# Layer 1's experts: from all eight on every row to the two chosen, on ranked tiles of 128 rows

## The chip, the cores and the metric

One NeuronCore of a Trainium2 chip runs the whole program. The metric is the device time of one execution in microseconds (us). Five engines work side by side and wait for each other through semaphores: TensorE (PE, matmuls), VectorE (DVE), ScalarE (ACT), GpSimd (POOL) and SyncE (SP, which mostly issues DMAs). Sixteen DMA engines move data between device memory (HBM) and the on-chip SBUF.

## What is computed

Two transformer layers on x of shape [2, 2048, 256], float32. Layer 0 is softmax attention with 16 heads of 16, then a mixture of 16 experts with limited capacity. Layer 1 is a linear attention, and then the block of which this change rewrites one half:

```
qkv = x @ W_qkv + b_qkv                    # W_qkv [256, 768]
attn_out = softmax(q k^T / 4) v            # 16 heads of 16, 2048 keys
gate = softmax(x @ W_gate + b_gate)        # 8 experts
top_g, top_i = top_k(gate, 2)
combine = sum(one_hot(top_i) * top_g)      # zero for 6 of the 8 experts
expert_out = einsum('bsd,edf->bsef', x, W_experts) + b_experts
return attn_out + einsum('bsef,bse->bsf', expert_out, combine)
```

Here x is the layernormed and modulated input h, and the result is added to the residual after a multiplication by a gate. No row is dropped in layer 1: each takes its two experts, however many rows choose the same one.

## The kernel before, in words

The 4096 rows are 32 tiles of 128 (NT), or 8 groups of 512 (N = B * GPB: two batches of four groups). The program is a row of blocks, each ended by a barrier of all engines: the projection of layer 0 (`project_layer0`), its attention (`softmax_attention`), its experts (`finish_layer0`), the linear attention, then `project_layer1_ffn` and the second `softmax_attention` (called with `last=True`).

`project_layer1_ffn` is the block that changes. Per group of 512 rows PE computes the logits of the gate (L1881), q and k (L1887, into the four banks of `qk_ps`), v (L1892), the biases of the experts weighted by the shares (L1898, L1903), and then for each of the four tiles all eight experts, in pairs of 512 columns (L1918). To keep float32 accuracy in the one-pass format (fp32r), each pair takes three products (high by high, high by low, low by high) for each half of the 256 inputs: 96 matmuls of 512 columns a group. DVE multiplies each expert's result by its share and adds it to `acc` (L2005, 32 a group), POOL multiplies by the gate of the residual and adds to x (L1865, L1867). The next group's layernorm is turned (`ln_tensor`, L141) before the last tile. ACT and DVE split q and k in a high and a low part (L175, L180), and SP stores them (`split_store`, L195) and v (`store_values`, L203) in HBM; at the last four groups SP also loads ahead the first keys (L322) and queries (L312) of the attention.

After the last group come `first_maxima` on PE (L252) and `take_first_maxima` on DVE (L261): 48 steps of two matmuls of 512 columns (50 rows each) and a maximum over 1024 columns, on a ring of two. They give the row maxima with which the attention starts.

`softmax_attention` runs 32 steps (two batches, four head groups, four query groups) of 16 key tiles. Per key tile PE does 4 score matmuls (L803), 4 for the maxima two steps ahead (L791) and 8 for the values (L818), ACT 4 exponentials (L873), DVE 2 maxima (L892). POOL is free but for adding the finished attention rows to x (L768, L770).

`finish_layer0` already has a form of what the change brings: rows scattered in HBM by expert with indirect DMAs on POOL (L1139), then 32 items of 256 rows. Each is loaded by SP (L1116, ring of four), turned by PE (L1221), shifted by ACT (L1317), multiplied (L1230, L1239) with weights at fixed addresses, scaled by DVE and stored; the linear attention gathers the rows again (L1513).

## Time and profile before

| | |
|---|---|
| median of 3 runs | 3696.02 us (3692.02 to 3698.27) |
| profiled execution, its own time | 3697.96 us |
| its span, first to last instruction | 3696.2 us |
| PE busy | 3494.7 us (95%) |
| DVE busy | 3144.4 us (85%) |
| ACT busy | 2532.1 us (69%) |
| POOL busy | 355.3 us (10%) |
| mean granted clock of PE | 0.957 of full speed |

Busy time is per engine; engines overlap, so the numbers don't add up to the span. The changed block runs from 2034.9 us to 2422.5 us of the span; the second attention fills the rest.

### The profile page before, as it was taken

Reading aid. Unit: us, or ns where it says so; the run is one execution under the profiler, and the core shown is the slowest. Engines: PE = TensorE matmul, PEld = TensorE weight load, DVE = VectorE, ACT = ScalarE, POOL = GpSimd, SP = SyncE. Lnnn points to the kernel's source line nnn. Section 1 sums busy time; section 2 is a strip of 40 time slices with the busy share of each in tenths; the row PEclk is TensorE's granted clock in tenths of the full one; section 3 lists DMA queues with packets and bytes.
Section 4 is the critical chain, followed back from the end, with each engine's and each line's share of the span. In section 5 each row is a group of like instructions: output and inputs, shape, how many; then the busy total and the mean of one; then the engine's idle time right before and its main releaser. Section 6 shows DMA issues by size and latency. Waiting matters only on the chain. (4 is left out here: it accounts for less than half of the span.)

```text
span 3696.2 us, 75111 instructions
## 1 busy us (share of the span) xinstructions
PE 3494.7 (95%) x29968; PEld 1634.9 (44%) x29968; DVE 3144.4 (85%) x4194; ACT 2532.1 (69%) x4681; POOL 355.3 (10%) x271
## 2 busy tenths in 40 slices
PE   9899999999999998677898899889999999999998
PEld 5433333333333333565777677533333333333333
DVE  8899999999999992524666676899999999999993
ACT  3188888888888886232322333168888888888887
POOL 4410000000000000341221121100000011000001
PEclk9699999999999999798999899789999999999999
DMA  9442020211202003152000325121220212202001
GB/s 258 121 137 38 14 42 15 37 31 26 37 20 37 14 11 99 63 188 82 27 23 12 91 57 104 41 42 22 34 37 18 38 42 59 39 14 42 15 16 45
DMA packets 279102, 193.17 MB, mean 52 GB/s; under 512 B 202573, under 2 KB 234230, under 8 KB 274384
## 3 DMA queue, kind: packets, MB, share of 16 engines
q1 hardware_dynamic: 268896, 158.40, 20.1%
q0 software_dynamic: 8400, 28.91, 2.2%
q8 instruction: 213, 3.49, 0.4%
q10 hardware_dynamic: 1504, 1.64, 0.1%
q14 instruction: 89, 0.73, 0.1%
HBM read 107.54 MB, written 81.79 MB: 51 GB/s over the span
## 5 line engine op out<-in xcount | busy, mean ns | idle before, releaser
L873 ACT ACTIVATE att_l_probs<-att_l_s_ps 128x512 f32<-128x512 f32 x4096 | 2212.1, 595 | 303.5 <-PE att_l_s_ps L803 238.2
L892 DVE TENSOR_REDUCE att_in_part_max<-att_l_max_ps 128x2 f32<-128x1024 f32 x1952 | 2328.2, 1218 | 10.2 <-PE att_l_max_ps L791 9.8
L818 PE MATMUL att_l_o_ps<-att_l_probs,att_l_v_sb 128*17 128x256 f32 x16384 | 1272.4, 386 | 0.9 <-ACT att_l_probs L873 0.9
L803 PE MATMUL att_l_s_ps<-att_in_q_sb,att_in_k_sb 50*128 50x512 f32 x2048 | 759.2, 447 | 9.0 <-DVE att_l_o_ps L909 9.0
L803 PE MATMUL att_l_s_ps<-att_in_q_sb,att_l_k_sb 50*128 50x512 f32 x2048 | 741.9, 448 | 0.1
L791 PE MATMUL att_l_max_ps<-att_l_k_sb,att_in_q_sb 50*128 50x512 f32 x2048 | 725.9, 444 | 0.0
L791 PE MATMUL att_l_max_ps<-att_in_k_sb,att_in_q_sb 50*128 50x512 f32 x1856 | 666.7, 449 | 0.0
L818 PEld LDWEIGHTS att_l_o_ps<-att_l_probs,att_l_v_sb 128*17 128x17 f32 x16384 | 279.6, 95 | 720.7 <-issue 377.0
L803 PEld LDWEIGHTS att_l_s_ps<-att_in_q_sb,att_in_k_sb 50*128 50x128 f32 x2048 | 312.3, 186 | 443.2 <-ACT att_l_probs L873 415.2
L803 PEld LDWEIGHTS att_l_s_ps<-att_in_q_sb,att_l_k_sb 50*128 50x128 f32 x2048 | 307.9, 185 | 433.7 <-ACT att_l_probs L873 401.0
L791 PEld LDWEIGHTS att_l_max_ps<-att_l_k_sb,att_in_q_sb 50*128 50x128 f32 x2048 | 291.8, 185 | 5.9 <-DVE att_in_part_max L892 5.9
L791 PEld LDWEIGHTS att_l_max_ps<-att_in_k_sb,att_in_q_sb 50*128 50x128 f32 x1856 | 267.1, 186 | 5.6 <-DVE att_in_part_max L892 5.4
L2005 DVE SCALAR_TENSOR_TENSOR ffn_acc<-ffn_qk_ps,ffn_comb,ffn_acc 128x256 f32<-128x256 f32 x256 | 123.9, 484 | 59.5 <-PE ffn_qk_ps L1918 54.1
L898 DVE STREAM_TRANSPOSE att_l_o_sb<-att_l_o_ps 128x512 f32<-128x512 f32 x64 | 45.2, 706 | 102.1 <-PE att_l_o_ps L818 102.1
L768 POOL TENSOR_TENSOR att<-att,all_gates 128x1024 f32<-128x1024 f32 x7 | 16.6, 2371 | 1190.3 <-DMA att<-att_rows 1190.3
L1134 POOL MEMSET post_ones<- 128x128 bf16 x1 | 0.2, 204 | 1218.6 <-POOLq L71 1218.6
L1428 DVE TENSOR_TENSOR post_hid<-post_act_gate,post_zT_ps 128x256 f32<-128x256 f32 x32 | 13.5, 422 | 110.6 <-ACT post_act_gate L1324 110.6
L1918 PE MATMUL ffn_qk_ps<-ffn_w_hi,ffn_h_hi 128*128 128x512 f32 x256 | 102.7, 401 | 0.0
L1918 PE MATMUL ffn_qk_ps<-ffn_w_hi,ffn_h_lo 128*128 128x512 f32 x256 | 101.2, 395 | 0.0
L1918 PE MATMUL ffn_qk_ps<-ffn_w_lo,ffn_h_hi 128*128 128x512 f32 x256 | 101.0, 395 | 0.0
L160 ACT ACTIVATE ffn_ln_hT<-ffn_ln_zT,all_modv 128x512 f32 (+1 forms) x18 | 13.0, 774 | 126.8 <-PE ffn_ln_zT L141 126.8
L1317 ACT ACTIVATE post_slot_hT<-post_y_ps,all_modv 128x256 f32<-128x256 f32 x64 | 32.5, 560 | 88.4 <-PE post_y_ps L1221 88.4
(238 smaller groups left out, 2945.8 us busy)
## 6 DMA issues: line engine op xcount, KB each, us to landing
att_in_q_sb<-q_hi SPq DMA_DIRECT2D x256, 64.0 KB
att_in_q_sb<-q_lo SPq DMA_DIRECT2D x128, 72.0 KB
att_l_v_sb<-v_rows SPq DMA_DIRECT2D x16, 544.0 KB, 15.2
att_in_k_sb<-k_hi SPq DMA_DIRECT2D x32, 256.0 KB, 10.0
att_l_k_sb<-k_hi SPq DMA_DIRECT2D x32, 256.0 KB, 9.8
slot_rows<-att_l_zeros POOLq DMA_DIRECT2D x8, 1024.0 KB, 13.6
att_rows<-att_l_o_div SPq DMA_DIRECT2D x256, 32.0 KB, 1.9
post_rows<-slot_rows SPq DMA_DIRECT2D x32, 256.0 KB, 3.1
```

The lines of the kernel that those rows point to most:

```text
L160: nc.scalar.activation(dst, ln.zT[:, half], ACT.Identity, bias=shift, scale=scale).then_inc(ln.h_ready, 1)
L768: nc.gpsimd.tensor_tensor(att, att, gate, ALU.mult).then_inc(att_scaled, 1)
L791: ins = nc.tensor.matmul(max_ps[:, r, half], q_sb[rows, j % QR, pair, tile * P:(tile + 1) * P], k_sb[j // GPB % 2][rows, pair, part * G:(p ...
L803: nc.tensor.matmul(s_ps[:, c % SB], k_sb[j // GPB % 2][rows, pair, u * P:(u + 1) * P], q_sb[rows, j % QR, pair], start=True, stop=True).th ...
L818: last = nc.tensor.matmul(o_ps[32 * h:32 * h + AUG, cols], v_sb[:, j // GPB % 2, u, h * AUG:(h + 1) * AUG], probs[:, u % 2, h, cols], star ...
L873: nc.scalar.activation(probs[:, u % 2, h], s_ps[:, c % SB], ACT.Exp, scale=float(HD) ** -0.5).then_inc(exp_done, 1)
L892: nc.vector.reduce_max(part_max[:, j % 2, k], max_ps[:, r], AX.X).then_inc(slot_taken, 1)
L898: nc.vector.transpose(o_sb[:].rearrange("p k c -> p (k c)"), o_ps[:]).then_inc(o_copied, 1)
L1317: nc.scalar.activation(slot_hT[:, i % 2, half], rT_ps[:, i % 2, half], ACT.Identity, bias=m.modv[:, 0, 2, half, b:b + 1], scale=m.modv[:, ...
L1428: nc.vector.tensor_tensor(hid[:, i % 2], act_gate[:, i % 2], gf_ps[:, i % 2, 1], ALU.mult).then_inc(hid_ready, 1)
L1918: last = nc.tensor.matmul(qk_ps[:, pair], h[:, slot * KH + kh, t * P:(t + 1) * P], w[:, kh, pair * 2 * D:(pair + 1) * 2 * D], start=(kh == ...
L2005: nc.vector.scalar_tensor_tensor(acc[:, t], qk_ps[:, e // 2, (e % 2) * D:(e % 2 + 1) * D], comb[:, t, e:e + 1], acc[:, t], ALU.mult, ALU.a ...
```

## The change

- The dense expert loop, its split weights, `acc`, `comb` and the bias product go. All layernormed rows are kept (`z_all`). The loops over groups are written out. q and k are split straight from PSUM, with their bias, on a double buffer of `parts`.
- Per batch (16 tiles), the logits are gathered, the two experts chosen (`choose`), and counted with matmuls (`count`: 1 + 32 in bf16). `positions` gives each expert whole tiles of 128 rows (at most 40 tiles a batch, `TILES`), and each chosen row its place. `experts_of_tiles` writes the expert of each tile in `which`.
- POOL scatters the rows of a batch with 32 indirect DMAs to `slot_rows`.
- 40 items of two tiles follow (20 a batch). SP loads an item, PE turns it, ACT shifts it, and PE multiplies it by the expert of its tile. The expert is read from `which` into a register of PE (`value_load`), which then addresses weights and bias. The bias enters as a product with a matrix of ones. The products are plain float32 (`w_exp` is no longer split). ACT copies the result, SP stores it in `tile_out`. The items of batch 0 run beside the first maxima, one every two steps from step 7; those of batch 1 behind them.
- In the second attention POOL gathers the two rows of each token, one indirect DMA per two key tiles (64 in all), and per group of 512 rows multiplies by the shares, adds the two, multiplies by the gate and adds to x. DVE's last additions wait for that.
- In the first attention `slot_rows` is zeroed with 10 DMAs instead of 8.

The core of the diff:

```
 in softmax_attention, POOL, last=True:
+                for i in range(B * GPB):
+                    b, tile = i // GPB, i % GPB * TPG
+                    xs = m.x[:, i * TPG:(i + 1) * TPG]
+                    if i > 0:
+                        pool.wait_ge(moe_added, i)
+                    for k in range(2):
+                        for t in range(TPG):
+                            pool.wait_ge(exp_done, (2 * (2 * TPG * i + k * TPG + t) + 4) * HG)
+                            nc.gpsimd.indirect_dma_start(out=got[:, k, t], in_=io.tile_out, ...)
+                    pool.wait_ge(got_in, (i + 1) * 16 * 2 * TPG)
+                    nc.gpsimd.tensor_tensor(got[:], got[:], share, ALU.mult).then_inc(got_step, 1)
+                    nc.gpsimd.tensor_tensor(got[:, 0], got[:, 0], got[:, 1], ALU.add)...
+                    nc.gpsimd.tensor_tensor(got[:, 0], got[:, 0], gate, ALU.mult)...
+                    nc.gpsimd.tensor_tensor(xs, xs, got[:, 0], ALU.add).then_inc(moe_added, 1)
 in softmax_attention, DVE, before the last additions:
+                dve.wait_ge(moe_added, B * GPB)
 in project_layer1_ffn, SP:
+            for n in range(N):
+                store_parts(n, b, q)
+                store_values(sync, io, va, v_copied, v_stored, n, b, q)
+                if n == 0:
+                    sync.dma_start(w_exp[:], io.w_exp).then_inc(exp_loaded, 16)
+                if n == GPB: ... load_keys(sync, io, ai, ai.k[0], 0, 0)
+                elif n > GPB: load_queries(sync, io, ai, 0, n - GPB - 1)
+            for r in range(2):
+                sync.wait_ge(stored[r], N // 2 * 16 * 4 * NPART)
+            for i in range(RING):
+                load(i)
+            for i in range(ITEMS):
+                if i == ITEMS_B + RING:
+                    store_shift(sync, io, ai, 0, 0)
+                sync.wait_ge(y_copied, i + 1)
+                sync.dma_start(by_item(io.tile_out)[i], y[:, i % RING])...
+                if i + RING < ITEMS:
+                    load(i + RING)
 PE:
+            def product(i):
+                ...
+                experts = [pe.value_load(which[0:1, b, c + t:c + t + 1], min_val=0, max_val=E1 - 1) for t in range(ITEM)]
+                pe.wait_ge(shift_ready, (i + 1) * KH)
+                if i >= 2:
+                    pe.wait_ge(y_copied, i - 1)
+                for t in range(ITEM):
+                    nc.tensor.matmul(out_ps[:, i % 2, t], ones_r[:], bias[:, ds(experts[t] * D, D)], start=True, stop=False)
+                    for kh in range(KH):
+                        last = nc.tensor.matmul(out_ps[:, i % 2, t], slot_hT[:, i % 2, kh, t * P:(t + 1) * P],
+                                                w_exp[:, kh, ds(experts[t] * D, D)], start=False, stop=(kh == KH - 1))
+                last.then_inc(out_ready, 1)
+            def item(i):
+                if i == 0:
+                    turn_item(0)
+                if i + 1 < ITEMS and (i + 1) % ITEMS_B:
+                    turn_item(i + 1)
+                product(i)
+            for n in range(N):
+                gate(n)
+                queries_keys(n)
+                if n == GPB:
+                    count(0)
+                if n + 1 < N:
+                    turn_normed(n + 1)
+                project_values(n)
+            pe.wait_ge(lo_ready, N * 4)
+            first_maxima(nc, pe, ai, qk_ps, beside)    # count(1) at k = 1, item(0) at k = 7, item(1) at k = 9, ...
+            turn_item(ITEMS_B)
+            for i in range(ITEMS_B, ITEMS):
+                item(i)
 DVE, per group n:
+                take_logits(n); if n + 1 < N: normalize(n + 1)
+                if n == GPB: choose(0)
+                if n == N - 1: choose(1)
+                for a in range(4): split_lo(n, a)      # waits hi_ready of ACT's split_hi
+                if n == GPB: positions(0); experts_of_tiles(0)
+                if n + 2 < N: statistics(n + 2)
+                take_values(n)
 POOL:
+            for b in range(B):
+                pool.wait_ge(put_ready, b + 1)
+                for k in range(2):
+                    for t in range(TPB):
+                        nc.gpsimd.indirect_dma_start(out=io.slot_rows, in_=z_all[:, b * TPB + t], ...)
```

(Several DVE lines are joined here with semicolons, and arguments cut with "...".)

## Rows read from the trace of the kernel before

**Rows 1.** Windows (span, busy us and instructions per engine, clock, DMA share, GB/s): the changed block.
```profile
2034.90:2050.00 15.10, 1.94 (x9) 1.57 (x9) 3.35 (x13) 1.80 (x4) 7.21 (x3) 0.50 0.55 201
2050.00:2363.80 313.80, 307.21 (x1314) 232.21 (x1316) 222.15 (x618) 99.99 (x172) 53.39 (x31) 0.98 0.34 77
2363.80:2422.50 58.70, 37.10 (x96) 13.37 (x94) 55.31 (x54) 0.67 (x1) 5.20 (x3) 0.51 0.01 1
```
**Rows 2.** Groups by line (count, busy us, mean ns, idle before): PE, 2089 to 2128 us.
```profile
L1918 PE MATMUL ffn_qk_ps<-ffn_w_hi,ffn_h_hi 128*128 128x512 f32 x34 | 13.4, 395 | 0.0
...
L1887 PE MATMUL ffn_qk_ps<-ffn_ln_hT,ffn_w_qkv 128*128 128x512 f32 x16 | 7.1, 598 | 0.0
L1892 PE MATMUL ffn_v_ps<-ffn_w_qkv,ffn_ln_hT 128*128 128x256 f32 x16 | 3.6, 379 | 0.0
...
L1881 PE MATMUL ffn_ln_zT<-ffn_w_gate,ffn_ln_hT 128*128 128x8 f32 x16 | 1.8, 251 | 0.0
L141 PE MATMUL ffn_ln_zT<-all_ident,ffn_ln_z 128*128 128x128 f32 x8 | 1.0, 273 | 0.0
```
**Rows 3.** DMA queues (packets, MB, share of 16 engines): 2128 to 2206, then 2206 to 2363 us.
```profile
q1 hardware_dynamic: 6496, 5.31, 29.5%
...
q1 hardware_dynamic: 14126, 13.42, 40.1%
```
**Rows 4.** Timeline of ACT in layer 0's projection: the root of each group (two of seven).
```profile
64.26 0.30 ACT L148 ACTIVATE qkv_ln_std<-qkv_ln_mv,all_eps 128x4 f32<-128x4 f32 x1 [1.22 <-DVE qkv_ln_mv L119]
75.93 0.30 ACT L148 ACTIVATE qkv_ln_std<-qkv_ln_mv,all_eps 128x4 f32<-128x4 f32 x1 [1.22 <-DVE qkv_ln_mv L119]
```
**Rows 5.** Windows: scatter alone, then scatter with layer 0's items.
```profile
1560.00:1570.00 10.00, 0.00 (x0) 0.00 (x0) 0.00 (x0) 0.00 (x0) 7.72 (x8) 0.50 0.24 86
1570.00:1580.00 10.00, 3.06 (x11) 2.54 (x12) 0.00 (x0) 2.27 (x5) 7.56 (x9) 0.50 0.66 208
1580.00:1590.00 10.00, 8.61 (x46) 7.28 (x45) 2.65 (x5) 4.44 (x9) 7.56 (x9) 0.98 0.68 240
```
**Rows 6.** Timeline of ACT at the block's start: its first instruction and what it waited for.
```profile
2045.42 0.30 ACT L148 ACTIVATE ffn_ln_std<-ffn_ln_mv,all_eps 128x4 f32<-128x4 f32 x1 [17.10 <-DMA ffn_sp_parts<-in_w_exp]
```
**Rows 7.** Groups by line: maxima on DVE in the block; POOL's sums; DVE beside POOL.
```profile
L261 DVE TENSOR_REDUCE att_in_part_max<-ffn_qk_ps 128x2 f32<-128x1024 f32 x48 | 54.7, 1211 | 0.6 <-PE ffn_qk_ps L252 0.6
L1865 POOL TENSOR_TENSOR ffn_acc_g<-ffn_acc,all_gates 128x1024 f32<-128x1024 f32 x8 | 18.8, 2355 | 44.3 <-DVE ffn_acc L2005 44.3
L1018 DVE TENSOR_TENSOR ffn_rt_logits<-ffn_rt_p,ffn_rt_mx 128x32 f32<-128x32 f32 x8 | 14.8, 1854 | 0.3
```
**Rows 8.** DMA issues (count, KB each, us to landing): the items' loads and stores.
```profile
post_rows<-slot_rows SPq DMA_DIRECT2D x32, 256.0 KB, 3.1
slot_out<-post_y SPq DMA_DIRECT2D x32, 256.0 KB, 2.3
```
**Rows 9.** Timeline of PE in layer 0's items.
```profile
1592.72 0.66 PE L1221 MATMUL post_y_ps<-all_ident,post_rows 128*128 128x128 f32 x4 [0.47 <-DMA post_rows<-slot_rows]
1593.21 1.89 PE L1230 MATMUL post_zT_ps<-post_slot_hT,post_w_gf 128*128 128x256 f32 x8
...
1596.58 0.66 PE L1221 MATMUL post_y_ps<-all_ident,post_rows 128*128 128x128 f32 x4 [0.61 <-DMA post_rows<-slot_rows]
```
**Rows 10.** Timeline in layer 0's projection: a step of the maxima at full clock.
```profile
115.09 0.50 PE L252 MATMUL qkv_qk_ps<-att_in_k_sb,att_in_q_sb 50*128 50x512 f32 x2
115.52 0.38 PE L556 MATMUL qkv_ln_zT<-qkv_cs,qkv_wmod 128*128 128x2 f32 x2
```
**Rows 11.** One line's instructions (ns min/median/max): POOL's gathers, with their register move.
```profile
L1158 POOLq MOVE  x8: 29/29/29, 1646.8 to 1650.5; - x8
L1158 POOL DMA_INDIRECT next_z_all<-slot_out,all_get_at x8: 1002/1002/1083, 1647.6 to 1656.8; - x8
```
**Rows 12.** Windows: maxima with other products beside (layer 0), then a stretch of the second attention.
```profile
150.00:180.00 30.00, 30.00 (x86) 16.73 (x86) 25.98 (x27) 1.02 (x1) 17.98 (x7) 0.50 0.01 2
...
2956.80:3049.20 92.40, 92.40 (x908) 33.42 (x906) 92.31 (x98) 81.50 (x151) 11.21 (x6) 1.00 0.15 42
```

More of the change, by code:

```diff
@@ new lines, in turn_item @@
+            def turn_item(i):
+                pe.wait_ge(item_loaded[i % RING], 16 * (i // RING + 1))
+                if i >= 2:
+                    pe.wait_ge(shift_ready, (i - 1) * KH)
+                elif i == 0:
+                    pe.wait_ge(logits_taken, N)
+                else:
+                    pe.wait_ge(count_read, B)
+                for t in range(ITEM):
+                    for half in range(KH):
+                        last = nc.tensor.transpose(rT_ps[:, i % 2, half, t * P:(t + 1) * P], rows[:, i % RING, t, half * P:(half + 1) * P], m.ident[:])
+                last.then_inc(turned, 1)
@@ new lines, in item, with beside @@
+            def item(i):
+                if i == 0:
+                    turn_item(0)
+                if i + 1 < ITEMS and (i + 1) % ITEMS_B:
+                    turn_item(i + 1)
+                product(i)
+            def beside(k):
+                if k == 1:
+                    count(1)
+                if k >= MAX_FIRST and (k - MAX_FIRST) % 2 == 0 and (k - MAX_FIRST) // 2 < ITEMS_B:
+                    item((k - MAX_FIRST) // 2)
+            pe.wait_ge(loaded, 16 * 8)
+            pe.wait_ge(ones_set, 3)
@@ new lines, in copy_item @@
+            def copy_item(i):
+                act.wait_ge(out_ready, i + 1)
+                if i >= RING:
+                    act.wait_ge(item_stored[i % RING], 16 * (i // RING))
+                nc.scalar.activation(y[:, i % RING], out_ps[:, i % 2], ACT.Copy).then_inc(y_copied, 1)
+            act.wait_ge(loaded, 16 * 8)
+            root(0)
+            modulate(0)
+            act.wait_ge(bias_set, 2)
+            act.wait_ge(bias_loaded, 32)
+            for row in (0, BROWS // 2):
+                nc.scalar.activation(bias[row:row + 1], b_raw[row:row + 1], ACT.Copy).then_inc(bias_hi, 1)
@@ new lines, in _ @@
+            statistics(0)
+            normalize(0)
+            statistics(1)
+            dve.wait_ge(loaded, 16 * 8)
+            dve.wait_ge(ones_set, 3)
+            for n in range(N):
+                take_logits(n)
+                if n == GPB - 1:
+                    lower_logits(0)
+                if n == N - 1:
+                    lower_logits(1)
+                if n + 1 < N:
+                    normalize(n + 1)
+                if n == GPB:
+                    choose(0)
+                if n == N - 1:
+                    choose(1)
+                for a in range(4):
+                    split_lo(n, a)
+                if n == GPB:
+                    positions(0)
+                    experts_of_tiles(0)
+                if n + 2 < N:
+                    statistics(n + 2)
+                take_values(n)
+                if n == 0:
+                    low = slice(BROWS // 2, BROWS // 2 + 1)
+                    dve.wait_ge(bias_hi, 2)
+                    nc.vector.tensor_tensor(bias[low], b_raw[low], bias[low].bitcast(F32), ALU.subtract).then_inc(bias_lo, 1)
+                    dve.wait_ge(bias_lo, 1)
@@ L2011, with beside, value_pairs @@
+            def beside(k):
+                if k == 1:
+                    positions(1)
+                    experts_of_tiles(1)
+            take_first_maxima(nc, dve, ai, qk_ps, beside)
+def value_pairs(n):
+    return (1, 0) if n == GPB else (0, 1)
 class State:
```

469 lines of the change are left out of this document (291 added, 178 removed).

## The prediction

> **What bounds the kernel now.** I first looked at the windows of the changed block [rows 1]: 15.1 us of start, 313.8 us of groups in which PE is busy for 307.2 at a clock of 0.98, and 58.7 us of first maxima with PE at half clock and DVE full. So the groups are bound by PE, the maxima by DVE. The groups by line show what PE does in 39 us [rows 2]: three forms of L1918, some 13 us each in overlapping records, fill most of it; the rest is q and k 7.1, v 3.6, gate 1.8, turning 1.0. In the second attention PE and DVE are both full (92.4 and 92.3 of 92.4 us), POOL nearly idle; its 1274 us should stay.
>
> **The groups.** All of L1918, the bias product and their waits go. What stays of PE's work is 7.1 + 3.6 + 1.8 + 1.0 = 13.5 us a group [rows 2], 108 us for eight. DVE's share (about 8 us of layernorm, low parts and values) and ACT's (about 4.5) lie beside it. I add 3 us because PE starts cold, and 2 + 2 us at the groups 4 and 7, where `choose` (about 6 us on DVE) goes before the low parts and the counts need PE for 3 us.
>
> What was hidden is the traffic. Two groups' stores took 29.5% of 78 us of the 16 engines, 11.5 us a group; the next 157 us held four groups' stores and the first keys and queries in 63 us, so these two cost 17 [rows 3]. Layer 0's projection stores the same amounts and turns over every 11.7 us [rows 4]: that pace is possible. Here 8 x 11.5 + 17, some 5 us for the 2 MB of expert weights, now loaded after group 0, and the scatter of batch 0 must pass. Scatter alone is 0.24 of the engines at 7.7 calls in 10 us of POOL [rows 5]: 32 calls make 10 us of traffic and occupy POOL for 41. In all 124 us, starting with the first low parts at about 2054: the queue is empty at about 2180 while PE alone would be done at 2163. As `parts` is a double buffer, group n waits for the stores of n - 2; I put 7 us of waiting on PE. At the start ACT waited until 2045.4 for the load of w_exp [rows 6]; it now waits for 0.75 MB of w_qkv and small tables only: 3 us earlier. Groups: 2047 + 108 + 3 + 4 + 7 = 2169, against 2363.8.
>
> **Maxima and the items of batch 0.** Steps 0 to 6 take 7 x 1.21 = 8.5 us [rows 7]. At step 7 PE asks for item 0, which SP may load only when all stores have landed (about 2180), 3.1 us after its issue [rows 8]: start at about 2183, a wait of 5 us in the middle of the maxima. The scatter is done by then (positions at about 2120, plus 41).
>
> The array's work of an item is known from layer 0's items: 0.6 for four transposes, 1.89 for eight float32 records of 256 columns [rows 9]; two bias products of one pass add 0.24 (estimate from 395 ns for 512 columns in overlapped records, some 0.23 from start to start, halved) : 2.7 us. Two steps of maxima add 2 x 0.43, from start to start [rows 10]: 3.6 us a slot, more than DVE's 2.42, so DVE no longer bounds this stretch.
>
> But an item has work that no row shows: two `value_load`s, which bring the expert's number from SBUF into a register of PE, and six matmuls whose address is computed from it. Bounds for a load: a register move of POOL took 29 ns, an indirect DMA of POOL, which reads 128 indices from SBUF and writes descriptors, 1.0 us [rows 11]; a whole store through the DMA takes 2.3 [rows 8]. It is nearest to the second, with less to do: I take 0.8. For an address I take three moves, 0.09 us; below that nothing, above it 0.4. The sequencer passes 908 + 906 records in 92.4 us [rows 12], 0.051 us each at most. An item has 28 records (1.43 us), so the sequencer needs 1.43 + 1.6 + 6 x 0.09 = 3.6 us, and with eight records and the ring of the maxima 4.2. Both are above the array's 2.7 and 3.6, and as the sequencer runs ahead the larger counts, not the sum. 20 x 4.2 = 84, and the steps 46 and 47 take 1: until 2268.
>
> The page "DMA: Bandwidth & Descriptors" of the Trainium skill gives in "Latency and other measured facts" a floor of some 600 ns for such a load. No run here shows it; as an estimate by that figure each item would be 0.4 us shorter and the whole 16 us, near 3611.
>
> **The items of batch 1.** Their scatter starts some 7 us after the groups (choose, count, positions beside step 1) and takes 41: ready at about 2218, long before 2268. A restart of 2.5 us (nothing is turned ahead over the change of batch), then 20 x 3.6 = 72: 2343. Loads must keep up: the ring of four and a turn of one item ahead leave two periods, 7.2 us, for copy 0.6, two issues 0.9 and landing 3.1. Layer 0's items waited 0.5 us each for their loads at a period of 3.9 [rows 9], but there the turn is two ahead. 512 KB an item is 2.3 us of traffic at the 208 to 240 GB/s that layer 0's mix reached [rows 5]: no bound. Last copy, store and the block's end: 0.6 + 0.4 + 2.3 + 3.6 = 7, so the attention starts at about 2350 instead of 2422.5: 72.5 us earlier.
>
> **The second attention.** POOL gets 64 gathers of 1.3 us and per group 4.7 (double of L1865, estimate) + 3 x 2.4 = 12 us of sums [rows 7], all in the first 130 of 512 key tiles: some 22 us in each 39 us step, so it keeps up, and DVE's added wait at the end is met 900 us before. Gathers of 8 MB in 320 us fit beside a DMA share of 0.15 [rows 12]. The danger is DVE, which is full: a DVE instruction of 0.19 us that reads two SBUF tiles took up to 2.1 beside POOL's sums (mean 1.85 in [rows 7]). In the attention only the division and the row maxima's small steps are of this kind; maxima from PSUM run undisturbed: the stretch with POOL busy for 11 us still has PE and DVE full [rows 12]. The last gather of a group is released behind key tile 1 of a step, the sums run from tile 3 to 8, the division is at tile 2, the small steps from tile 8 on. Cost: nothing below, 8 x 4.7 = 38 above; I take 2.
>
> The Trainium skill has a rule for this: "SBUF — State Buffer", section "Who interferes with whom", says that a DVE instruction with two SBUF inputs and a GpSimd instruction that reads SBUF shut each other out for a whole instruction. The trace agrees (2.1 us against 0.19). By it the cost is zero if the order above holds, and up to the 38 us if the sums slide over the division.
>
> **Sum.** 3697.96 (the profiled execution's own time) - 72.5 + 2 = 3627; the median of the runs is 2 us below that execution, within what I can tell. A change under 0.2% (7 us) can't be told from none in this kernel. The layer 0 attention's two added zeroing DMAs lie beside 1200 us of work: nothing.
>
> **Rivals.**
> A. *The array bounds the items*: loads cost 0.2 us or less and hide behind the queue. Slots 3.6 and 2.8: 28 us less, 3599. For it: matmuls are issued far ahead. Against: a load stops the sequencer, and two stand in every item.
> B. *The items wait*: for SP's ring or for traffic while POOL scatters batch 1 (layer 0's mix used 0.66 to 0.68 of the engines [rows 5]), or the low parts drain later. Items at 4.7 on average, or 30 us more in all: 3660. For it: layer 0's 0.5 us waits.
> C. *Slower*: the register loads cost more than all eight experts saved. The gain of 71 us is spent when an item takes 1.8 us more on average, that is when two loads and six addresses cost 3.9 instead of 2.1 us. With loads like a store's way through the DMA (2.3 each) the sequencer needs 1.43 + 4.6 + 0.5 = 6.5, 7.1 with maxima: 2.9 x 40 = 116 more, 3743. With it goes the clock: in layer 0's maxima PE stayed at 1.2 GHz for 30 us though busy throughout [rows 12], and starved of instructions it could do so here. Against: layer 0's items brought it to 0.98 within 10 us [rows 5].
> D. *The gathers aren't hidden*: the sums collide with DVE's division in each group, 38 us less gain: 3665.
>
> **Chances.** Forecast (3605 to 3650): 0.50. A 0.18, B and D together 0.13, C 0.14, and 0.05 for costs that just eat the gain, within 7 us. Range 3588 to 3692: it leaves out C's slower part and little of A. Faster 0.81, same 0.05, slower 0.14.
>
> **What would show it.** Groups' period 13.5 to 14.5 us at full clock; DMA share over 0.85 in them; PE's first item at about 2183; item period 3.6 behind the maxima, with PE's idle time called issue, not a wait for ACT or a load; the second attention 1274 us long with 39.4 us steps also in its first quarter. The forecast is wrong if an item takes over 5 us, if PE's clock is 0.5 in the items, or if the steps of the attention's first quarter are over 40 us.

## The result, and the profile after

The changed kernel took 3631.8 us (median of four runs, 3627.4 to 3637.8) against 3696.9 for the kernel before (four runs, 3692.0 to 3698.3): ratio 0.983, 95% interval 0.981 to 0.985. It is faster by 65 us; the prediction said 3627. The profiled execution of the changed kernel took 3629.9 us with a span of 3628.1.

The windows of the changed block answer to [rows 1] (columns as there; the start, 2029.1 to 2042, is left out): groups, first maxima up to the first item, two items at low clock, the rest of batch 0 with the maxima, batch 1.

```profile
...
2042.00:2161.70 119.70, 112.21 (x473) 74.61 (x473) 72.45 (x279) 41.59 (x60) 31.49 (x32) 0.94 0.84 225
2161.70:2184.50 22.80, 8.87 (x49) 4.90 (x49) 14.39 (x25) 0.00 (x0) 8.80 (x9) 0.57 0.92 217
2184.50:2203.90 19.40, 18.90 (x59) 11.39 (x59) 4.86 (x5) 5.74 (x11) 14.76 (x16) 0.62 0.57 191
2203.90:2271.10 67.20, 67.20 (x304) 40.96 (x302) 40.48 (x40) 26.41 (x50) 7.86 (x8) 1.00 0.49 151
2271.10:2346.60 75.50, 67.30 (x282) 46.04 (x280) 2.72 (x3) 30.50 (x61) 0.71 (x1) 0.95 0.43 133
```

The block takes 317.5 us instead of 387.6, so 70 us went here. The groups went from 313.8 to some 120 us, the maxima with batch 0 beside them take 110 instead of 58.7, and batch 1's items add 75 that were not there.

The groups by line on PE, 2044 to 2083 us, answer to [rows 2]; behind them the roots of two successive groups in ACT's timeline.

```profile
L1987 PE MATMUL ffn_qk_ps<-ffn_hT,ffn_w_qkv 128*128 128x512 f32 x48 | 23.3, 641 | 0.0
L1999 PE MATMUL ffn_v_ps<-ffn_w_qkv,ffn_hT 128*128 128x256 f32 x42 | 9.6, 379 | 0.0
L1978 PE MATMUL ffn_zT_ps<-ffn_w_gate,ffn_hT 128*128 128x8 f32 x39 | 5.3, 271 | 0.0
```

```profile
...
2057.57 0.30 ACT L2086 ACTIVATE ffn_std<-ffn_mv,all_eps 128x4 f32<-128x4 f32 x1 [1.02 <-DVE ffn_mv L2167]
...
2070.56 0.30 ACT L2086 ACTIVATE ffn_std<-ffn_mv,all_eps 128x4 f32<-128x4 f32 x1 [1.03 <-DVE ffn_mv L2167]
```

In 39 us there are now three groups instead of one, a group every 13.0 us. Q and k (L1987), v (L1999), the gate (L1978) and the turning of the normed rows are all that PE does.

An item beside the maxima, PE's timeline (start, us from first start to last end, line; "x4" are four records):

```profile
...
2235.21 0.73 PE L252 MATMUL ffn_qk_ps<-att_in_k_sb,att_in_q_sb 50*128 50x512 f32 x4
2235.87 0.66 PE L2028 MATMUL ffn_zT_ps<-all_ident,ffn_parts 128*128 128x128 f32 x4
2236.46 0.38 PE L2046 MATMUL ffn_v_ps<-ffn_bias,ffn_ones_r 64*128 x1
2236.77 1.13 PE L2048 MATMUL ffn_v_ps<-ffn_w_exp,ffn_hT 128*128 x4
2237.83 0.39 PE L2046 MATMUL ffn_v_ps<-ffn_bias,ffn_ones_r 64*128 x1
2238.15 1.13 PE L2048 MATMUL ffn_v_ps<-ffn_w_exp,ffn_hT 128*128 x4
2239.21 0.73 PE L252 MATMUL ffn_qk_ps<-att_in_k_sb,att_in_q_sb 50*128 50x512 f32 x4
```

From one L252 to the next, a slot of one item and two steps of the maxima, are 4.00 us, and this repeats without variation from 2203.9 to 2267.9. An item of batch 1 is the same without L252 and takes 3.18 us (2279.32 to 2282.50). A bias product (L2046) begins 0.31 us before the expert products (L2048), and these hold the array for 1.06. Expert products, a tile's four records, take the same time in every item.

The register loads, which no row of before showed, are done by PE's sequencer, which issues all of PE's instructions (PEldq in the rows). Here they are by their line (count: duration in ns, least, median, most), 2203 to 2268 us:

```profile
L2041 PEldq TENSOR_LOAD <-ffn_which x33: 296/300/425, 2203.0 to 2266.8; - x33
L2041 PEldq FUSED_REGOPS  x33: 151/151/151, 2203.3 to 2267.2; - x33
L2041 PEldq SEQ_ASSERT  x33: 18/18/18, 2203.5 to 2267.4; - x33
```

and those of an expert product's address:

```profile
...
L2048 PEldq ALU_OP  x33: 32/32/36, 2203.9 to 2267.7; - x33
L2048 PEldq FUSED_REGOPS  x33: 46/51/51, 2204.0 to 2267.8; - x33
```

The three instructions of a `value_load` last 0.30, 0.15 and 0.02 us, 0.47 together; with the gaps between them the next one begins 0.64 us behind it (e4 below). Each address takes one register instruction of 0.03 or 0.05 us: two of each an item in these rows and two of 0.05 at the bias's line (L2046), six in all, 0.26 us together.

The second attention takes 1281.5 us (2346.6 to the span's end), 7.8 more than before. DVE's turning of a finished step's result comes every 39.4 us, as before, but for two intervals of 31: 41.5 and 46.0 us. What happens in the second, by the timelines of POOL, DVE and PE (the idle time ahead in brackets) and by windows:

```profile
2684.46 3.60 POOL L782 TENSOR_TENSOR att_l_got<-att_l_got,all_top_p 128x2048 f32<-128x2048 f32 x1 [12.88 <-DMA att_l_got<-tile_out,all_get_at]
...
2693.06 2.35 POOL L789 TENSOR_TENSOR all_x_res<-all_x_res,att_l_got 128x1024 f32<-128x1024 f32 x1
```

```profile
...
2689.05 1.51 DVE L277 CAST att_in_max_parts<-att_in_row_max 128x16 fp32r<-128x16 f32 x1
...
2691.62 1.40 DVE L280 TENSOR_TENSOR att_in_max_parts<-att_in_row_max,att_in_max_parts 128x16 fp32r<-128x16 f32 x1
...
2699.73 1.22 DVE L920 TENSOR_REDUCE att_in_part_max<-att_l_max_ps 128x2 f32<-128x1024 f32 x1 [0.91 <-PE att_l_max_ps L819]
```

```profile
...
2691.75 0.51 PE L819 MATMUL att_l_max_ps<-att_in_k_sb,att_in_q_sb 50*128 50x512 f32 x2 [0.54 <-DVE att_in_part_max L920]
...
2694.20 0.79 PE L819 MATMUL att_l_max_ps<-att_in_k_sb,att_in_q_sb 50*128 50x512 f32 x2 [0.74 <-DVE att_in_part_max L920]
```

```profile
...
2693.00:2705.00 12.00, 11.26 (x66) 3.70 (x64) 8.18 (x9) 5.65 (x11) 2.35 (x1) 0.57 0.02 3
2705.00:2714.00 9.00, 9.00 (x89) 3.20 (x85) 8.79 (x9) 7.80 (x15) 0.00 (x0) 1.00 0.09 24
```

POOL waited 12.9 us for the group's last gathers (12.8 at step 4), 1.9 in the groups without such a stretch, as the loads of the next keys and values fill the DMA engines (share 0.87 from 2669 to 2689). So POOL's sums ran beside the small steps of DVE on the row maxima, which took 1.5 and 1.4 us instead of 0.16. PE waited for the maxima, its granted clock went from 2.4 to 1.2 GHz, and DVE in its turn waited for PE until 2705.

### The profile page after: what moved, and what is told of

Its sections match the earlier page's. It is cut to its first block and busy times, and to the rows that moved or that the text cites. A ratio compares the mean times of both kernels' runs of the same rounds, so it can differ in the third digit from the quotient of the medians.

```text
span 3628.1 us, 74192 instructions
## 1 busy us (share of the span) xinstructions
PE 3426.2 (94%) x29722; PEld 1564.4 (43%) x29722; DVE 3010.1 (83%) x3880; ACT 2536.0 (70%) x4688; POOL 514.7 (14%) x405
## 5 line engine op out<-in xcount | busy, mean ns | idle before, releaser
L1457 DVE TENSOR_TENSOR post_hid<-post_act_gate,post_zT_ps 128x256 f32<-128x256 f32 x32 | 13.5, 421 | 108.5 <-ACT post_act_gate L1353 108.5
L2048 PE MATMUL ffn_v_ps<-ffn_w_exp,ffn_hT 128*128 x320 | 96.5, 426 | 0.0
L261 DVE TENSOR_REDUCE att_in_part_max<-ffn_qk_ps 128x2 f32<-128x1024 f32 x48 | 56.5, 1217 | 45.5 <-PE ffn_qk_ps L252 45.5
L1692 ACT ACTIVATE lin_o_sb<-lin_o_ps 128x512 f32<-128x512 f32 x32 | 19.1, 597 | 98.9 <-PE lin_o_ps L1587 98.9
L776 POOL DMA_INDIRECT att_l_got<-tile_out,all_get_at x64 | 64.6, 1010 | 152.7 <-ACT att_l_probs L901 149.6
L1776 DVE TENSOR_TENSOR lin_masked<-lin_qk_ps,all_triu 128x1024 f32<-128x1024 f32 x64 | 75.0, 1212 | 6.6 <-PE lin_qk_ps L1578 6.6
```

Source lines behind the costliest of these rows:

```text
L261: nc.vector.reduce_max(ai.part_max[:, k // MAXI, k % MAXI], ps[:, k % 2 * 2:k % 2 * 2 + 2], AX.X).then_inc(ai.slot_taken, 1)
L776: nc.gpsimd.indirect_dma_start(out=got[:, k, t], out_offset=None, in_=io.tile_out, in_offset=bass.IndirectOffsetOnAxis(ap=m.get_at[:, b, k ...
L1692: nc.scalar.activation(o_sb[:], o_ps[:], ACT.Copy).then_inc(o_copied, 1)
L1776: nc.vector.tensor_tensor(masked[:, t % 2, banks].rearrange("p r e n -> p (r e) n"), qk_ps[:, banks].rearrange("p r (e n) -> p (r e) n", n=P),
L2048: last = nc.tensor.matmul(out_ps[:, i % 2, t], slot_hT[:, i % 2, kh, t * P:(t + 1) * P], w_exp[:, kh, ds(experts[t] * D, D)], start=False, ...
```

## The experiments

Three sets ran, each on its own chip with the kernel before beside it: e1 to e4, e5 to e8, e9 to e12. In the first two the kernel before took 3696.3 and 3698.1 us, in the third 3764.2, so e9 to e12 are compared with each other alone.

**e1: gathers 8 key tiles earlier.**

```diff
- pool.wait_ge(exp_done, (2 * (2 * TPG * i + k * TPG + t) + 4) * HG)
+ pool.wait_ge(exp_done, max(1, 2 * (2 * TPG * i + k * TPG + t) - 4) * HG)
```

> Changed kernel with each gather released 8 key tiles earlier (the last of a group behind tile 10 of a step instead of tile 2 of the next). Theory (the sums slide): in the changed kernel the second attention took 1281.5 us instead of 1273.7 because at its steps 4 and 8 the keys' and values' loads held up the last gathers of a group (landing waited for 12.8 us instead of 1.9), so POOL's sums slid over DVE's small steps on the row maxima (1.4 us instead of 0.16), in step 8 with PE's clock falling to 1.2 GHz for some 9 us. Then here the sums run in tiles 11 to 15, nothing slides, all steps are 39.4 us, and the second attention is 1273.8 us: 3624 us in all. Rival (traffic): it is the gathers' traffic that delays the keys and values themselves; then steps 4 and 8 stay at 41.5 and 46 us or others take their place, 3630 to 3632. Rival (sums cost wherever they are): the stretch spreads over all eight groups, each step 0.5 to 1 us longer, 3628 to 3632.

All intervals are as in the kernel before (39.4 us, the last two 36.9 and 35.3): from the first to the last turning it is 1214.7 us, against 1214.6 there, where the changed kernel had 1223.2. DVE's small steps over the whole attention, first here, then in e5 (the changed kernel again):

```profile
...
L934 DVE TENSOR_TENSOR att_l_o_div<-att_l_o_sb,att_l_inv 128x256 f32<-128x256 f32 x32 | 13.6, 426 | 1.1
...
L277 DVE CAST att_in_max_parts<-att_in_row_max 128x16 fp32r<-128x16 f32 x31 | 5.1, 165 | 0.0
```

```profile
...
L934 DVE TENSOR_TENSOR att_l_o_div<-att_l_o_sb,att_l_inv 128x256 f32<-128x256 f32 x32 | 13.6, 426 | 1.1
...
L277 DVE CAST att_in_max_parts<-att_in_row_max 128x16 fp32r<-128x16 f32 x31 | 7.5, 242 | 0.0
```

The division (L934) costs the same in both, 426 ns; only the small steps were stretched. POOL waited 1.9 to 2.8 us for its gathers in all eight groups. So the first theory holds and both rivals fall. The whole took 3630.8 us (3627.5 to 3633.1), but the changed kernel itself did not run in this set: it has 3631.8 in the first measurement and 3641.6 in e5. So the totals settle nothing here; the trace does, as the stretch from the first to the last turning is 8.5 us shorter in it.

**e2: expert weights loaded in the block before.**

```diff
+ sync.dma_start(m.w_exp[:], io.w_exp).then_inc(m.exp_loaded, 16)   # linear attention's block
...
- if n == 0:
-     sync.dma_start(w_exp[:], io.w_exp).then_inc(exp_loaded, 16)
```

> Changed kernel with the 2 MB of expert weights loaded at the start of the linear attention's block (DMA share 0.08 there) instead of behind group 0 of the changed block; their place in SBUF serves before that as layer 0's output tiles of the items. Theory (the groups are bound by traffic): the share was 0.84 at 221 GB/s over the groups and the first item was loaded only when all stores had landed; 2 MB less are 9.5 us at that rate, so group 7 and the first item come 8 to 10 us earlier: 3622 us. Rival (PE and the chain of an iteration bound the groups, the prediction's 13.5 us a group): 0 to 2 us earlier, 3630. The prediction had put these 2 MB at 5 us.

It took 3636.5 us (3632.1 to 3643.4). From the block's first root to the first item there are 153.3 us, in the changed kernel 149.3 and in its variants e1, e3 and e4 152.0 to 152.7. The same stretch takes 149.3 to 154.1 us over the traces in which only other parts differ, so nothing came earlier: the theory fell. The windows of e2 show why; the first covers the groups in which the weights used to land:

```profile
2050.00:2085.00 35.00, 35.00 (x137) 23.00 (x138) 20.54 (x53) 13.63 (x19) 0.00 (x0) 0.92 0.64 157
...
2137.00:2163.00 26.00, 20.13 (x73) 12.34 (x72) 5.93 (x14) 6.79 (x11) 18.65 (x19) 0.91 1.00 287
```

Early in the groups the DMA engines have room (share 0.64, and 0.71 in the changed kernel with the weights, 2042.6 to 2077.6), and a group comes every 13.0 us with the weights or without. They are full only from group 5 on, when the first keys and the scatter come on top of the stores, and by then the weights are gone from the queue: over the 26 us in which the scatter starts the share is 0.82 in the changed kernel and 0.81 here. So the traffic of the block can't be summed over the whole stretch; what counts is what is due together with that burst.

**e3: constant experts; e4: twice the register loads.** In e3 most tiles take the wrong expert.

```diff
- experts = [pe.value_load(which[0:1, b, c + t:c + t + 1], min_val=0, max_val=E1 - 1) for t in range(ITEM)]
+ experts = [(c + t) // 5 for t in range(ITEM)]                                                  # e3
+ for t in range(ITEM): pe.value_load(which[0:1, b, c + t:c + t + 1], min_val=0, max_val=E1 - 1)  # e4, added
```

> Changed kernel without the register loads: tile number c takes expert c // 5, so the experts of most tiles are wrong; the same products, all addresses constants. Theory (the array bounds the items): loads (0.30 + 0.15 us each in the records) and addresses lie behind the array's 4.00 us (beside the maxima) and 3.18 us; both periods stay, 3630 to 3632 us. Rival (the prediction's: PE's sequencer bounds the items): it loses 2 x 0.47 + 6 x 0.08 = 1.4 us an item and the array's 3.6 and 2.7 us, as predicted, come out: 40 x 0.45 = 18 us less, 3614 us.

> Changed kernel with two further register loads in each item, whose values nobody uses. A load takes 0.30 us and the register work and check behind it 0.15 + 0.02 in the changed kernel's records: 0.94 us more for the sequencer per item. Theory (array bounds, the sequencer has some slack): the sequencer's sum 28 records x 0.051 + 2 x 0.47 + 6 x 0.08 = 2.85 us against 3.18 alone and some 3.3 against 4.00 beside the maxima; with 0.94 more, 3.8 and 4.2: 20 x 0.6 + 20 x 0.2 = 16 us more, 3648 us. Rival (sequencer is already the bound, the prediction's): all of it, 40 x 0.94 = 38 us more, 3669 us. Rival (loads go entirely behind the queue of issued matmuls): 0 to 2 us more, 3632.

e3 took 3631.4 us (3621.7 to 3639.1), and both periods stayed to the hundredth, 4.00 and 3.18:

```profile
...
2320.33 0.60 PE L2028 MATMUL ffn_zT_ps<-all_ident,ffn_parts 128*128 128x128 f32 x4
2320.86 0.38 PE L2046 MATMUL ffn_v_ps<-ffn_bias,ffn_ones_r 64*128 64x256 f32 x1
...
2323.51 0.60 PE L2028 MATMUL ffn_zT_ps<-all_ident,ffn_parts 128*128 128x128 f32 x4
```

So loads and addresses cost nothing here, and the prediction's statement that PE's sequencer bounds the items is wrong. e4 took 3652.6 us (3645.2 to 3663.8), 21 more than e3 beside it. Batch 1's items came every 3.85 us on average (2319.5 to 2346.5, seven), the slots every 4.36 (2214.4 to 2275.5, fourteen). PE then stands in every second slot between turning and bias product:

```profile
...
2232.03 0.66 PE L2028 MATMUL ffn_zT_ps<-all_ident,ffn_parts 128*128 128x128 f32 x4
2233.25 0.38 PE L2048 MATMUL ffn_v_ps<-ffn_bias,ffn_ones_r 64*128 x1 [0.57 <-issue]
...
2236.66 0.66 PE L2028 MATMUL ffn_zT_ps<-all_ident,ffn_parts 128*128 128x128 f32 x4
2237.24 0.38 PE L2048 MATMUL ffn_v_ps<-ffn_bias,ffn_ones_r 64*128 x1
```

Within an item the loads follow each other without a wait, here the two added ones, 0.64 us apart (2322.98 and 2323.62):

```profile
L2043 PEldq TENSOR_LOAD <-ffn_which x2: 301/302/303, 2323.0 to 2323.6; - x2
```

At 3.85 us the sequencer is the bound, and without the two added loads (2 x 0.64, not the 0.94 that the expectation took from the durations) it would need 2.6: 0.6 less than the array's 3.18. That is the slack in which the loads hide. The theory's 16 us was near the 21 measured.

**e5 and e12: the changed kernel again.**

> The changed kernel itself, once more, beside its variants on one chip. Theory (noise ahead of the block): the 5.8 us by which the changed block began earlier in the first trace are no part of the change; the first root of the block, 2035.3 us there, came at 2043.6, 2042.8, 2040.4 and 2039.6 in four variants whose code up to it is the same or nearly so; here it is between 2036 and 2044. Rival (they belong to the change): 2035 to 2036. Theory on the second attention: steps 4 and 8 are longer than 39.4 us again, by 3 to 13 us together. Time 3628 to 3636 us.

> The changed kernel a third time, as the measure for e9 to e11 on their chip. 3628 to 3642 us; second attention's steps 4 and 8 longer than 39.4 us by 3 to 13 us together; first root between 2035 and 2044 us; items 26 and 27 late.

e5 took 3641.6 us (3639.9 to 3644.2), ratio 0.985 (0.983 to 0.986): 6 us outside what was expected. The first root of the block came at 2042.5 us; over the seven traces of that speed whose code is the same up to it (the changed kernel, e1, e3, e4, e5, e7, e8) it lies between 2035.3 and 2044.1. So the 5.8 us by which the block began earlier in the first trace are within the spread between traces of the same code, and no part of the change: with the root 6.2 us behind the block's start, the block begins between 2029 and 2038 in these, and the kernel before had 2034.9. The stretched steps were there again, 41.6 and 45.8 us.

e12, on the chip of the third set, took 3747.6 us (3739.6 to 3752.8), ratio 0.995 (0.994 to 0.996), over 100 us outside what was expected; the kernel before was 66 us slower there than in e5's set. Steps 4 and 8 of the attention took 45.3 and 41.3 us, but the others up to the seventh took 40.0 to 40.4 too. There the first root came 61 us later than in e5, all of it lost in layer 0's experts and the linear attention, whose code is the same as in the kernel before. In the changed block DVE and ACT stood still while POOL scattered batch 1's rows; DVE's and ACT's timeline, the idle time ahead in brackets:

```profile
...
2287.64 0.60 ACT L2119 ACTIVATE ffn_parts<-ffn_v_ps 128x512 f32<-128x512 f32 x1 [14.62 <-remote]
...
2293.26 1.23 DVE L261 TENSOR_REDUCE att_in_part_max<-ffn_qk_ps 128x2 f32<-128x1024 f32 x1 [27.68 <-DMA lin_wo_w<-in_l_wo]
...
2303.79 0.56 ACT L2112 ACTIVATE ffn_hT<-ffn_zT_ps,all_modv 128x256 f32<-128x256 f32 x1 [15.55 <-remote]
```

PE had given the maxima at 2278.8, and DVE took them at 2293.3. The semaphore events name a DMA of another block as what ended DVE's wait, which can't be; the instruction that waited was not ready for another reason. POOL's calls took 0.98 us in e12 as in e5. What holds the engines there stays open. It is in the variants e9 to e11 too. From the first root to the attention's first turned result e12 took 401.4 us against 361.6 in e5, most of the gain: 12 of these 40 us lie ahead of the first item, 30 between it and the restart for batch 1, and behind that it was 2 faster.

**e6: gathers early, items from step 9, two value buffers.**

```diff
- MAX_FIRST = 7
+ MAX_FIRST = 9
- va = sb("va", [P, TPG, NH * AUG])
+ va = sb("va", [P, 2, TPG, NH * AUG])     # and v_stored per buffer
```

> Three edits of the changed kernel together: gathers 8 key tiles earlier (e1), items beside the maxima from step 9 instead of 7, and two buffers for the values on their way to memory, so that group 6's values don't wait for group 5's stores (15.9 us of DVE's wait in e2's trace). Theory: the attention's stretched steps go (3 to 13 us, 7 in the middle); of PE's wait of 5.6 us for the first item two maxima steps are taken out, which saves their 0.66 to 0.8 us each behind it; the second value buffer lets the maxima begin some 10 us earlier but the first item, which needs all stores landed, comes no earlier: 0 to 1 us. In all 8 to 10 us below the changed kernel on this chip, about 3622. Rival (the value buffer's wait was on the path): the first item comes 5 us or more earlier and it is 3616 or less. Rival (nothing but noise is left to gain): within 4 us of the changed kernel.

It took 3629.2 us (3628.2 to 3635.5), ratio 0.982 (0.981 to 0.983), against 3641.6 of the changed kernel beside it: 12 us less, a version that beats both. Of these, 8.6 are the attention's (1214.7 us from first to last turning against 1223.3). The second value buffer did what was said of it and no more: DVE took the first maximum 120.5 us behind the first root instead of 136.4, the first item 153.7 instead of 154.1. PE simply waited longer:

```profile
...
PEld ffn_zT_ps L2029 <- DMA ffn_parts<-slot_rows: 17.8, 2, 17.5
```

**e7: no bias products.** The experts' biases are missing in the output.

```diff
- nc.tensor.matmul(out_ps[:, i % 2, t], ones_r[:], bias[:, ds(experts[t] * D, D)], start=True, stop=False)
```

> Changed kernel without the bias's product in each tile: the experts' biases are left out of the output. Theory (the product takes 0.31 us of the array from start to start, not the 0.12 of the prediction): an item loses 0.62 us, its periods go from 4.00 to 3.4 and from 3.18 to 2.56: 40 x 0.62 = 25 us less, 3607 us. Rival (0.12 us each is its share and the rest is a gap of the array that another cause makes, which stays): 40 x 0.24 = 10 us less, 3622. Rival (the register loads, 2 x 0.47 us, and the sequencer's other work then become the bound, at 2 x 0.47 + 26 x 0.051 + 4 x 0.08 = 2.6 and with maxima 3.1 to 3.4): about as the theory, 3607 to 3610.

It took 3614.2 us (3606.8 to 3618.3), 27.5 less than e5: near the theory's 25. PE's timeline in batch 1:

```profile
...
2296.14 1.89 PE L2047 MATMUL ffn_v_ps<-ffn_w_exp,ffn_hT 128*128 x8
2297.87 0.60 PE L2028 MATMUL ffn_zT_ps<-all_ident,ffn_parts 128*128 128x128 f32 x4
2298.31 1.89 PE L2047 MATMUL ffn_v_ps<-ffn_w_exp,ffn_hT 128*128 x8
```

Eight expert records follow each other at 0.216 us and an item takes 2.17; with the bias 3.18, so a bias product costs (3.18 - 2.17) / 2 = 0.50 us. Now and then an item comes 1.2 us later; on average they take 2.68 (2295.7 to 2322.5, ten), and the slots 3.29 (2209.2 to 2261.9, sixteen). In the late items PE stands for 0.8 to 0.9 us between turning and product while the sequencer still works on the two register loads, once (2311.5) after a wait for the item's rows. So the loads no longer hide in full, as the last rival had it. But 2.6 us is not what the sequencer needs: undisturbed it passes an item in 2.15 (first load to first load, 2302.10 to 2304.25).

**e8: batch 0's scatter left out.** Its items read zeros, and batch 0's share of the output is wrong.

```diff
- for k in range(2):
+ for k in range(2 if b else 0):
```

> Changed kernel without the scatter of batch 0's rows (32 calls of 128 KB); its items read what stands in the rows, zeros, so batch 0's share of the output is wrong. Theory (from group 4 on the first item is bound by traffic: stores, keys and queries, and this scatter, at a DMA share of 0.85 to 1.0): 4.2 MB at 245 to 287 GB/s are 15 to 17 us; group 6's value wait goes, the maxima and the first item come 12 to 16 us earlier: 3617 us. Rival (SP's own issue of the stores and loads sets the pace, one at a time): 0 to 3 us earlier, 3630.

3635.3 us (two runs), 6 less than e5. The first item came 146.4 us behind the first root instead of 154.1. Six traces in which nothing ahead of the first item differs have 149.3 to 154.1, so the scatter holds the first item up by 3 to 8 us, not 15: the DMA share stays at 0.94 without it, but at 204 instead of 236 GB/s (57 and 64 us to the first item). The rest of its traffic probably went where the stores left room; no run shows that by itself. The theory's 12 to 16 us are wrong; the rival's upper end, 3 us, is not ruled out by this one trace.

**e9: the two bias products one behind the other.**

```diff
  for t in range(ITEM):
-     nc.tensor.matmul(..., bias[:, ds(experts[t] * D, D)], start=True, stop=False)
+     nc.tensor.matmul(..., bias[:, ds(experts[t] * D, D)], start=(t == 0), stop=False)
+ for t in range(ITEM):
      for kh in range(KH):
          last = nc.tensor.matmul(...)
```

> Changed kernel with the bias products of an item's two tiles issued one behind the other, before the four expert products; all else as it was. e7 showed that a bias product costs an item of batch 1 (3.18 - 2.17) / 2 = 0.50 us, though 0.12 would do for its columns. Theory (the change between kinds of products costs: each time the array goes from the float32 products to the weights of the ones and back): one such change of two goes, 0.38 us less per item, until the sequencer bounds it at 3.85 - 0.94 = 2.9 us (from e4): periods 3.18 to 2.9 and 4.00 to 3.65, 20 x 0.28 + 20 x 0.35 = 13 us less than the changed kernel on the same chip. Rival (the product itself costs 0.50 wherever it stands): periods stay, 0 to 1 us.

3732.1 us (3731.4 to 3735.3) against 3747.6 (3739.6 to 3752.8) for e12 beside it: 15 less. An item in PE's timeline:

```profile
...
2416.41 0.60 PE L2028 MATMUL ffn_zT_ps<-all_ident,ffn_parts 128*128 128x128 f32 x4
2416.94 0.50 PE L2046 MATMUL ffn_v_ps<-ffn_bias,ffn_ones_r 64*128 x2
2417.37 1.99 PE L2050 MATMUL ffn_v_ps<-ffn_w_exp,ffn_hT 128*128 x8
2419.20 0.60 PE L2028 MATMUL ffn_zT_ps<-all_ident,ffn_parts 128*128 128x128 f32 x4
```

The item takes 2.79 us, and a slot beside the maxima 3.60 instead of 4.00. Against e7's 2.17 the two bias products add 0.62: 0.50 for the first, as in e7, and 0.12 for the second, no more than its columns. So it is the change between the two kinds of product that costs, about 0.4 us there and back, not the product. The edit also leaves one product with `start=True` where there were two; that is not the cause, as e7's items have two such products and their eight records still follow each other at 0.216 us. The kinds differ in format (fp32r and float32) and in rows (64 and 128); which of the two costs was not separated.

On average the items come at 2.92 (2404.9 to 2434.2, ten). That is not the sequencer's bound: eight of these ten take 2.78 to 2.84, and the longest, 3.77, begins with a wait for the item's rows (PE's weight load at 2424.82 waited for that DMA); the register loads behind it then lie open. Undisturbed, the sequencer passes an item in 2.27 us (2427.14 to 2429.41).

**e10: the shift's store behind item 36.**

```diff
- if i == ITEMS_B + RING:
+ if i == ITEMS - RING:
      store_shift(sync, io, ai, 0, 0)
```

> Changed kernel with SP's store of the shift and its way back (store_shift) behind item 36 instead of ahead of item 24's store. Theory (SP's queue): in every trace of the changed kernel and its variants SP stands from 2286.9 to 2292.4 for the shift's round trip, the ring of four loads runs dry, and items 26 and 27 come at 4.7 and 6.6 us instead of 3.18, the next at 4.2, part of it at 1.2 GHz: with nothing in the way 1.5 + 3.4 + 1.0 = 6 us less than the changed kernel on the same chip, and no stretch below 2.4 GHz between the items 21 and 39. Rival (the loads wait for traffic, not for SP): 0 to 1 us. Rival (the attention's first product then waits for the late shift): the gain goes there.

SP's queue in the changed kernel, where the shift goes out and back between two items:

```profile
...
2286.89 0.50 SPq L292 DMA_DIRECT2D shift<-att_in_max_cols  x1
2289.64 2.81 SPq L299 DMA_DIRECT2D att_in_q_sb<-shift  x4
2292.49 0.45 SPq L1933 DMA_DIRECT2D tile_out<-ffn_parts  x1
```

e10 took 3741.3 us (3740.1 to 3747.9), 6 less than e12, as expected, though the ranges of the single runs overlap. Its items come at 3.18 us without exception from 2391.3 to 2445.3, where e12 has one of 4.73, one of 5.61 and one of 3.86: 4.7 us by the traces.

**e11: all five.**

> All together: gathers 8 key tiles earlier, items from step 9, two value buffers (as e6), the bias products in pairs (e9) and the shift's store behind item 36 (e10). Theory: the gains are on one chain and add up: 12 (e6, on its chip) + 13 + 6 = 31 us below the changed kernel on this chip, near 3602 to 3608. Rival (a faster item makes another wait: the ring of loads, then traffic): 18 to 25 below, 3610 to 3618.

3723.0 us (3722.2 to 3728.0), ratio 0.989 (0.988 to 0.991), 24.6 below the changed kernel on its chip and 41 below the kernel before. That is 6 less than the sum and within the rival's 18 to 25; the absolute 3602 to 3618 had been expected for the speed of the first sets. The attention's steps 4 and 8 take 39.7 and 39.4 us, but its intervals 6 and 7 took 45.5 and 43.5, with PE's granted clock at 0.89 and 0.92. From first to last turning the attention took 1225.6 us against e12's 1226.9, so the early gathers brought 1.3 us here instead of 8.6, which is what the sum lacks. DVE's small steps took 0.17 us there, so it is not the collision of the changed kernel; the cause is open, and in this set no other kernel ran with the early gathers.

## Why the prediction came out right, step by step

Its total was 5 us below the median. Where the time would be saved held; the engine that it named as the bound of the items did not, and errors of up to 7 us in single stretches had opposite signs. That the total came so near is in part luck.

- **Start.** 3 us earlier was said; the first root stands 6.2 us behind the block's start instead of 10.5 [rows 6]: 4.3.
- **Groups.** 13.5 us a group; measured 13.0. Their end, by the first maxima product, was put 134 us behind the block's start and came at 132.7. The 7 us of waiting for stores was right in size and nearly so in place: it is PE's wait for DVE at group 7 (4.4 and 2.8 us), where DVE stood up to 14.4 us for the value buffer. The 5 us for the weights within the traffic was wrong: e2 shows no gain without them, within a spread of 5 us between traces.
- **First item.** Put at 148 us behind the block's start, measured 155.4. This step failed by 7 us. SP issued its load 148.5 us behind the block's start instead of 145, and the landing was priced at 3.1 us from layer 0 [rows 8], but the four ring loads went out at a DMA share of 0.92 behind the last queries, and the first took 6.9 (2177.6 to 2184.5). e8 puts the scatter's part of the delay at 3 to 8 us, e2 the weights' at none.
- **Items of batch 0.** 20 x 4.2 = 84 and 1 us were said; from the first item to that of batch 1 it took 86.6, with 4.00 us a slot and two of 8.6 and 6.7, mostly at 1.2 GHz.
- **Items of batch 1.** 2.5 + 72 + 7 us, 81.5, were said; measured 75.5 from the restart to the attention (1.9 to the first product, 68.6 for the items, 5.0 behind). A period of 3.18 instead of 3.6 gave back 8 us, and the shift's round trip in SP's queue took 5 to 6. The prediction had looked at SP's ring for bandwidth and landing, and had not listed what else stands in that queue.
- **The named bound.** "Both are above the array's 2.7 and 3.6" is the statement that failed: e3 took all loads and addresses out and the periods stayed at 3.18 and 4.00. Both sides of the comparison were mis-sized. The sequencer, when nothing holds it, passes an item in 2.27 us (e9), not 3.6: two loads take 2 x 0.64 instead of 2 x 0.8, and the 28 records with their addresses 1.0 instead of 2.0. The larger error is thus the price of a record; 0.051 us was a bound from above [rows 12], worked out from a stretch that PE and DVE filled, and it went into the sum as the price. And the array needs 3.18, not 2.7: eight expert records take 1.73 instead of 1.89 and four transposes 0.44 instead of 0.6, but two bias products 1.01 instead of 0.24 (e7), and the mean of overlapped records [rows 2] could not show that changing the kind of product costs. That the forecast periods, 3.6 and 4.2, lie near the measured 3.18 and 4.00 is luck, as they were worked out for the wrong engine. Rival A had the right engine with the wrong price: its 2.8 and 3.6 would have given 3599. (The prediction quoted a floor of some 600 ns for a load from the Trainium skill, "DMA: Bandwidth & Descriptors", "Latency and other measured facts". Here the load instruction itself took 0.30 us and a whole `value_load` 0.64.)
- **The second attention.** + 2 us was said, + 7.8 measured. Rival D had the mechanism, DVE's two-input instructions beside POOL's sums, but aimed at the division, which never met them. The prediction asked whether the gathers fit into the traffic on average (0.15), and not when the last one lands while the next keys are on their way: POOL waited 12.8 and 12.9 us for it, at steps 4 and 8. The order "sums from tile 3 to 8, small steps from tile 8 on" had no reserve against that. One of its own signs of being wrong, steps of over 40 us in the attention's first quarter, came true at these two of eight steps. Where DVE's small steps met POOL's sums they took 1.4 to 1.5 us instead of 0.16, and in e1, where they didn't meet, 0.16. The Trainium skill's rule in "SBUF — State Buffer", section "Who interferes with whom", that a DVE instruction with two SBUF inputs and a GpSimd instruction that reads SBUF shut each other out, fits the second of the two steps (L280); the first (L277) has one input, and for it the same section says that casts can enter a mode that takes the shared ports too. The prediction had quoted only the half on two inputs. Of the 6.6 us of step 8 the two stretched steps are 2.6; the other 4.0 fell while PE ran at 1.2 GHz.
- **Errors that met.** First item 7 late, batch 0's items 2 late, batch 1's 6 early; the attention 6 more, and the stretch ahead of the block 6 us less by chance. A repeat on another chip gave 3641.6 (e5), within the likeliest case's own range.

## What to carry to other kernels

Where a tail is mixed of small products of two kinds, count how often the array changes between them, and group by kind: here a change there and back cost about 0.4 us, a bias product of 256 columns itself 0.12. When a background engine is allowed beside a full one because their steps interleave, work out when its input lands at the worst moment, not on average, and leave it the widest gap; here 8 key tiles of lead took the stretched steps away. Look where the DMA engines are full before counting traffic: here moving 2 MB out of an earlier part of the same block bought nothing. And look at what else stands in a queue that feeds a ring: here a round trip of 5.6 us cost 5 to 6, as the ring ran dry. Where a bound from above is the only row for a price, carry it through the sum as a bound: here it named the wrong engine.

## What the runs showed of the hardware that was not expected

- A register load from SBUF by PE's sequencer took 0.30 us (median; now and then 0.4 to 0.6), with its register work and check one followed another at 0.64 us (e4), and two an item lay wholly behind queued products (e3 against the changed kernel: 4.00 and 3.18 us in both). Once the turning had waited for an item's rows, the loads behind it lay open and the item came 1 us late (e7, e9).
- The same kernel had a ratio of 0.983 in the first measurement, 0.985 in e5 and 0.995 in e12, on a chip on which the kernel before itself was 66 us slower than in e5's set. The traces show engines standing still there beside POOL's scatter, without a releaser that makes sense. What the change brought differed by 40 us between two sets, and why is open.
- After a gap of PE of 0.5 and 0.7 us in the attention the granted clock fell from 2.4 to 1.2 GHz and stayed there till 2705 although PE was busy throughout again; with that, 2.6 us of stretched DVE steps became 6.6.
